# A routed mixture's end: 39 of 47 blocks summed during the last blocks, eight added in DRAM with their weights

## What is computed

```python
scores = softmax(xt @ Wg.T)                     # xt = layernorm(x), (1024, 256); 16 experts
topi   = top_k(masked, 4)                       # masked: the best 2 of 4 groups of 4 experts
weights = scores at topi
combine[t, topi] += weights
h = silu(xt @ W1[e]) * (xt @ W3[e])             # inner size 176
expert_out[e, t] = h @ W2[e].T
y = sum over e of expert_out[e, t] * combine[t, e]
z = silu(xt @ Ws1.T) * (xt @ Ws3.T) @ Ws2.T     # shared part
x = x + y + z
```

## Time and profile before

| | us |
|---|---|
| median of 3 runs (lowest, highest) | 798.14 (797.76, 800.05) |
| the profiled execution's own time | 797.48 |
| its span | 795.5 |
| PE busy, share of the span | 709.1, 89% |
| DVE busy | 574.2, 72% |
| ACT busy | 444.4, 56% |
| POOL busy | 399.1, 50% |
| mean granted TensorE clock | 0.961 |

### The profile page before, as it was taken

The page is one execution under the profiler, slowest core; times in us unless marked ns, Lnnn a source line. Parts: engine busy times, 40 slices in busy tenths (PEclk is TensorE's granted clock), DMA queues, the critical chain, the costliest instruction groups (busy, mean ns, idle before and its releaser), DMA issues. The chain is left out here.

```text
span 795.5 us, 12267 instructions
## 1 busy us (share of the span) xinstructions
PE 709.1 (89%) x3946; PEld 555.8 (70%) x3946; DVE 574.2 (72%) x1072; ACT 444.4 (56%) x969; POOL 399.1 (50%) x334
## 2 busy tenths in 40 slices
PE   8598967999999997999999999999798699999950
PEld 3144433688888886899998988988687555788840
DVE  6999999744343367889898888888889667544436
ACT  3887754253443335777776767776642266555530
POOL 0699877245675543534353232233232477777720
PEclk9699999999999998999999999999999799999975
DMA  4746411110444501120211033000077122233327
GB/s 142 281 168 254 163 64 44 59 37 22 140 129 133 175 14 48 41 73 27 74 60 34 22 105 139 1 1 1 21 275 263 40 67 87 87 100 101 100 80 231
DMA packets 38823, 77.66 MB, mean 98 GB/s; under 512 B 5345, under 2 KB 20394, under 8 KB 37738
## 3 DMA queue, kind: packets, MB, share of 16 engines
q1 hardware_dynamic: 34088, 64.41, 23.6%
q0 software_dynamic: 4512, 12.33, 5.1%
q10 hardware_dynamic: 162, 0.14, 0.1%
HBM read 59.07 MB, written 17.79 MB: 97 GB/s over the span
## 5 line engine op out<-in xcount | busy, mean ns | idle before, releaser
L1184 PE MATMUL psum<-xT_hi,w_ring 128*128 128x512 f32 x272 | 91.2, 395 | 1.0 <-ACTq L285 0.7
L2483 ACT ACTIVATE a_p_exp<-psum,a_nmax 128x256 f32<-128x256 f32 x128 | 59.6, 471 | 57.4 <-DVE a_nmax L2652 57.4
L2582 POOL TENSOR_TENSOR a_rr<-a_ss,eps 128x8 f32<-128x8 f32 x32 | 6.6, 206 | 158.0 <-DVE a_ss L2633 158.0
L641 POOL TENSOR_TENSOR m_dbu<-m_du,m_b_all 128x1024 f32<-128x1024 f32 x31 | 73.7, 2398 | 9.5 <-DVE m_du L727 6.9
L735 DVE TENSOR_TENSOR_SCAN m_hst<-psum,m_dbu 128x1024 f32<-128x1024 f32 x32 | 73.0, 2283 | 0.0
L1963 POOL DMA_INDIRECT expert_rows<-y_rows,f_puts_i x47 | 54.3, 1155 | 32.0 <-ACT y_rows L1909 31.4
L1320 POOL TENSOR_TENSOR f_h_lo<-f_hid,f_h_hi 128x512 fp32r<-128x512 f32 x34 | 44.0, 1296 | 44.6 <-ACT f_h_hi L1294 44.0
L2346 PE MATMUL psum<-a_kT,a_qT 128*128 128x256 f32 x256 | 62.0, 386 | 1.4 <-ACT a_kT L2475 1.4
L387 PE MATMUL psum<-m_hc,ident 128*128 128x512 f32 x128 | 61.8, 606 | 0.0
L1184 PEld LDWEIGHTS psum<-xT_hi,w_ring 128*128 128x128 f32 x272 | 51.1, 188 | 11.9 <-issue 1.5
L1294 ACT ACTIVATE f_h_hi<-f_hid 128x512 fp32r<-128x512 f32 x34 | 21.4, 631 | 63.3 <-DVE f_hid L1428 45.3
(11 more groups left out here) (312 smaller groups left out, 2245.7 us busy)
## 6 DMA issues: line engine op xcount, KB each, us to landing
expert<-in_experts SPq DMA_DIRECT2D x16, 608.0 KB, 8.6
m_b_all<-b_rows SPq DMA_DIRECT2D x8, 1024.0 KB, 5.9
w_raw<-in_moe SPq DMA_DIRECT2D x20, 384.0 KB, 3.5
k_raw<-m_side SPq DMA_DIRECT2D x16, 256.0 KB, 2.0
a_keys<-k_raw SPq DMA_DIRECT2D x16, 256.0 KB, 2.6
norm_rows<-xn SPq DMA_DIRECT2D x8, 512.0 KB, 7.6
added<-expert_rows SPq DMA_DIRECT2D x16, 256.0 KB, 5.7
fold_in<-in_w_fold SPq DMA_DIRECT2D x8, 384.0 KB, 3.3
```

The source lines that it names most:

```text
L641: pool.tensor_tensor(dbu[:, k % DBU_RING, :, :], du[:, h, :, :], b_all[:, n:n + 1, :].to_broadcast([P, G, HALF]), ALU.mult).then_inc(dbu_r ...
L1184: mm = pe.matmul(dst, a[part], b[of], start=(k == 0 and i == 0), stop=(k == KD - 1 and i == 2), skip_group_check=True)
L2483: ins = act.activation(pe_[:, n % 2, m, :], bank(hh)[:, tile * L:(tile + 1) * L], ACT.Exp, bias=nmax[:, n % 2, m:m + 1], accum_out=rsum[:, ...
```

## The change

Four things, with their places in the new kernel:

- **Exp and the weights move into the loop.** ACT takes Exp after turn 3, DVE makes the weights after turn 4 (WEIGHTS_AT = 4). SP then writes the weights to a DRAM array, slot_weights.
- **Eight weight gathers.** In turns 6 to 13 POOL fetches, for each of the last eight blocks, one number for each of its 128 rows. Their indices come from `lasts_listed`, nine DVE instructions ahead of block 0, and one more in `rows_listed`.
- **The last eight blocks (39 to 46)** are scaled by these weights in the y_rows copy, and their scatters add into two DRAM arrays in turn, last_rows0 and last_rows1, at the token's row. A scatter waits until the one before it in the same array has landed. The rows of expert_rows and of the two arrays are zeroed in the attention, by eight DMAs of 1 MB (8.4 MB in all), ahead of the first six experts in SP's queue (`sums_cleared`).
- **The end.** The first 39 blocks' rows are read once their scatters have landed, one token tile (four picks, 512 KB) a DMA, into two buffers in turn, xn and parts. A buffer is refilled when its tile has been added. DVE adds two picks in each of turns 43 to 46, the other 24 behind the loop, each waiting for the one before. Then SP reads the two arrays, four DMAs each, and DVE adds them in eight instructions of 512 columns.

```diff
 GATHERS = 6
+LAST = 8
...
-ADDED = [(f"added{k}", [P, NT, DM], F32) for k in range(4)]
+ADDED = [(f"added{p}", [P, NT, DM], F32) for p in range(2)]
...
+        self.inputs = 16 * (16 + 4 + 2 * 2)
+
+    def sums_cleared(self, sp):
+
+        zeros = self.sh.zeros[:, :].bitcast(F32)
+        first = T * 3 + P * (NB1 - LAST)
+
+        def cleared(rows):
+            sp.dma_start(rows.rearrange("(t p) f -> p t f", p=P),
+                         zeros.unsqueeze(1).to_broadcast([P, rows.shape[0] // P, DM])).then_inc(self.experts_in, 16)
+
+        for k in range(4):
+            cleared(self.d["y_rows"][k * T:(k + 1) * T, :])
+        for p in range(2):
+            cleared(self.d["last_rows"][p][0:T, :])
+            cleared(self.d["last_rows"][p][first:first + LAST * P, :])
...
+    KEPT = NB - LAST
+    WEIGHTS_AT, PARTS_AT = 4, KEPT + 4
...
+        parts = [sh.xn, sh.tables["parts"]]
...
-            return len(range(r, NB, PUTS))
+            return len(range(r, KEPT, PUTS))
...
+                sp.wait_ge(weights_kept, 1)
+                sp.dma_start(d["slot_weights"].rearrange("(p r) w -> p (r w)", p=P),
+                             weights_of[:, :, :].rearrange("p k t -> p (k t)")).then_inc(weights_out, 16)
                 for r in range(PUTS):
                     sp.wait_ge(put[r], 16 * puts_of(r))
+                for t in range(NT):
+                    if t >= 2:
+                        sp.wait_ge(final, picks * (t - 1))
+                    sp.dma_start(parts[t % 2][:, :, :],
+                                 d["y_rows"][0:picks * T, :].rearrange("(k t p) f -> t p k f", p=P, k=picks)[t]).then_inc(part_in[t % 2], 16)
+
+                def sums(p, q):
+                    return d["last_rows"][p][2 * q * P:(2 * q + 2) * P, :].rearrange("(t p) f -> p t f", p=P)
+
+                sp.wait_ge(y_s, NB)
+                sp.wait_ge(last_put[0], 16 * lasts_of(0))
                 for q in range(NT // 2):
-                    for k in range(picks):
-                        at = k * T + 2 * q * P
-                        sp.dma_start(added[k][:, 2 * q:2 * q + 2, :],
-                                     d["y_rows"][at:at + 2 * P, :].rearrange("(t p) f -> p t f", p=P)).then_inc(added_in[q], 16)
+                    sp.dma_start(added[0][:, 2 * q:2 * q + 2, :], sums(0, q)).then_inc(added_first, 16)
+                sp.wait_ge(last_put[1], 16 * lasts_of(1))
                 for q in range(NT // 2):
-                    sp.wait_ge(final, 2 * picks * (q + 1))
+                    sp.dma_start(added[1][:, 2 * q:2 * q + 2, :], sums(1, q)).then_inc(added_in[q], 16)
+                for q in range(NT // 2):
+                    sp.wait_ge(final, picks * NT + NT // 2 + q + 1)
                     sp.dma_start(out.rearrange("(t p) f -> p t f", p=P)[:, 2 * q:2 * q + 2, :],
                                  x[:, 2 * q:2 * q + 2, :]).then_inc(stored, 16)
                 sp.wait_ge(stored, 16 * (NT // 2))
...
                 def block_out(i):
                     act.wait_ge(y_ps, i + 1)
-                    if i >= PUTS:
+                    j = i - KEPT
+                    if j >= PUTS:
+                        act.wait_ge(last_put[j % 2], 16 * ((j - PUTS) // 2 + 1))
+                    elif i >= PUTS:
                         act.wait_ge(put[i % PUTS], 16 * (i // PUTS))
-                    act.activation(y_rows[:, i % PUTS, :], y_bank(i)[:, 0:DM], ACT.Copy).then_inc(y_s, 1)
+                    if j < 0:
+                        act.activation(y_rows[:, i % PUTS, :], y_bank(i)[:, 0:DM], ACT.Copy).then_inc(y_s, 1)
+                    else:
+                        if j == 0:
+                            act.wait_ge(slot_weights, 16 * LAST)
+                        act.activation(y_rows[:, i % PUTS, :], y_bank(i)[:, 0:DM], ACT.Identity, scale=slot_weight[:, j:j + 1])\
+                            .then_inc(y_s, 1)
...
-                act.wait_ge(weighed, 1)
-                act.activation(ex[:, :, :], ex[:, :, :], ACT.Exp).then_inc(mix.ex_ready, 1)
+                    if i == WEIGHTS_AT - 1:
+                        act.wait_ge(weighed, 1)
+                        act.activation(ex[:, :, :], ex[:, :, :], ACT.Exp).then_inc(mix.ex_ready, 1)
...
                 def scatter(i):
                     pool.wait_ge(y_s, i + 1)
+                    j = i - KEPT
+                    if j >= 0:
+                        if j >= 2:
+                            pool.wait_ge(last_put[j % 2], 16 * (j // 2))
+                        pool.indirect_dma_start(d["last_rows"][j % 2], bass.IndirectOffsetOnAxis(last_i[:, j:j + 1], 0),
+                                                y_rows[:, i % PUTS, :], None, compute_op=ALU.add).then_inc(last_put[j % 2], 16)
+                        return
                     pool.indirect_dma_start(d["y_rows"], bass.IndirectOffsetOnAxis(puts_i[:, i:i + 1], 0),
                                             y_rows[:, i % PUTS, :], None).then_inc(put[i % PUTS], 16)
 
                     if i + GATHERS - 1 < NB:
                         gather(i + GATHERS - 1)
                     scatter(i)
+                    if WEIGHTS_AT + 2 <= i < WEIGHTS_AT + 2 + LAST:
+                        j = i - WEIGHTS_AT - 2
+                        if j == 0:
+                            pool.wait_ge(rows_ready, 4)
+                            pool.wait_ge(weights_out, 16)
+                        pool.indirect_dma_start(slot_weight[:, j:j + 1], None, d["slot_weights"],
+                                                bass.IndirectOffsetOnAxis(weight_i[:, j:j + 1], 0)).then_inc(slot_weights, 16)
...
+                def lasts_listed():
+
+                    last = slice(KEPT, NB)
+                    step(dve.tensor_scalar(whole_row, row, -(T - 1) / 2, 1.0 / T, ALU.add, ALU.mult))
+                    step(dve.tensor_scalar(whole_row, whole_row, MAGIC, None, ALU.add))
+                    step(dve.tensor_scalar(whole_row, whole_row, -MAGIC, None, ALU.add))
+                    step(dve.scalar_tensor_tensor(whole_row, whole_row, -float(T), row, ALU.mult, ALU.add))
+                    dve.tensor_tensor(last_i[:, :], whole_row, rows_f[:, last], ALU.add).then_inc(rows_ready, 1)
+                    step(dve.tensor_scalar(whole_tile, row, -(P - 1) / 2, 1.0 / P, ALU.add, ALU.mult))
+                    step(dve.tensor_scalar(whole_tile, whole_tile, MAGIC, None, ALU.add))
+                    step(dve.tensor_scalar(whole_tile, whole_tile, -MAGIC, float(1 - P * picks * NT), ALU.add, ALU.mult))
+                    dve.scalar_tensor_tensor(weight_i[:, :], row, float(picks * NT), whole_tile, ALU.mult, ALU.add)\
+                        .then_inc(rows_ready, 1)
...
+                def part_added(part):
+
+                    t, k = part // picks, part % picks
+                    if k == 0:
+                        dve.wait_ge(part_in[t % 2], 16 * (t // 2 + 1))
+                    else:
+                        dve.wait_ge(final, part)
+                    dve.scalar_tensor_tensor(x[:, t, :], parts[t % 2][:, k, :], weights_of[:, k, t:t + 1], x[:, t, :],
+                                             ALU.mult, ALU.add).then_inc(final, 1)
...
-                weights_picked()
-                for q in range(NT // 2):
-                    dve.wait_ge(added_in[q], 16 * picks)
-                    for k in range(picks):
-                        if k > 0:
-                            dve.wait_ge(final, 2 * (picks * q + k))
-                        for t in (2 * q, 2 * q + 1):
-                            dve.scalar_tensor_tensor(x[:, t, :], added[k][:, t, :], weights_of[:, k, t:t + 1], x[:, t, :],
-                                                     ALU.mult, ALU.add).then_inc(final, 1)
+                    if i == WEIGHTS_AT:
+                        weights_picked()
+                    if PARTS_AT <= i < NB:
+                        part_added(2 * (i - PARTS_AT))
+                        part_added(2 * (i - PARTS_AT) + 1)
+
+                for part in range(2 * (NB - PARTS_AT), picks * NT):
+                    part_added(part)
+                dve.wait_ge(added_first, 16 * NT // 2)
+                for p in range(2):
+                    for q in range(NT // 2):
+                        if p == 0:
+                            dve.wait_ge(final, picks * NT)
+                        else:
+                            dve.wait_ge(added_in[q], 16)
+                            dve.wait_ge(final, picks * NT + q + 1)
+                        xs = x[:, 2 * q:2 * q + 2, :].rearrange("p t f -> p (t f)")
+                        dve.tensor_tensor(xs, xs, added[p][:, 2 * q:2 * q + 2, :].rearrange("p t f -> p (t f)"), ALU.add)\
+                            .then_inc(final, 1)
...
+                sparse.sums_cleared(sp)
```

28 lines of the change are left out of this document (22 added, 6 removed).

## The result

| | before | after |
|---|---|---|
| median (lowest, highest) | 799.1 (797.76, 800.44) | 820.12 (816.97, 822.72) |
| runs | 4 | 4 |
| ratio, 95% interval | | 1.0282 (1.0249 to 1.0314) |
| profiled execution: own time, span | 797.48, 795.5 | 820.04, 818.2 |
| E, end of the last y_rows copy | 769.5 | 791.9 |

The change makes the kernel 21 us slower. The forecast said slower, by 7; its range ended at 812. The loop costs more than forecast and the tail gives nothing. The ratios in this document leave out an execution that lies over 1.5% above the fastest of its kernel, and only one does: the profiled one of weights_ahead (819.24).

A forecast was written before the change was run, and what follows sets the result against it. PE nearly fills the loop, and every microsecond saved in the tail is span. 1.4 + 2.5 + 6.5 - 3.2 = +7.2 on 797.48 gives 804.7, with half the 0.66 to the median 805.0 us; range 798 to 812.

The forecast's parts named there:

- step 3: Blocks 6 to 13: eight weight gathers on POOL, 0.97 us each plus gap, make PE wait for rows: +6.5 us.
- step 5: Tail: part reads in two buffers, then the two arrays' reads and adds, end at E+22.8 instead of E+26.0: -3.2 us.
- step 2: Block 4: making the weights on DVE delays b_hidT, for which PE waits: +2.5 us.
- step 4: Zeros, list operations, early reads, adds in the loop and scaling of y_rows are all covered: no cost.
- Exp into the loop: ACT after block 3: Exp and table loads start the next gate late, on the path to PE's down product: +1.4 us.
- steps 1 and 2: Exp with its table loads on ACT and the weights on DVE, blocks 3 and 4: together +3.9 us.
- the rival of a stretched POOL: Weight gathers starting under DVE's experts_lo cost 1.5 us each, 4.4 more in all: 809 us, chance 0.2.
- the bound of -8: Tail: with every read early DVE sets the pace, and the arrays' reads end it at about E+18.
- slow adding scatters: Last blocks: serialised adding scatters slower than 5.3 us lengthen the chain, past 6.6 the tail waits; at 8, 810; chance 0.1.
- A fast weight gather and the bound in the tail: Weight gathers on POOL nearly free and the tail gains 8 us: 793 with no gather delay, chance 0.1.

The follow-up runs named there:

- weights_ahead: The changed kernel with Exp and the weights made ahead of block 0, weight gathers where they are: 811.2 us, ratio 1.0141 to the kernel before.
- the filled pauses: The changed kernel with matmuls of zeros before block 4's down product and before the x_rows transposes of turns 9 to 15: 816.83 us.
- four_part_buffers: The changed kernel with four part buffers instead of two, so that four tiles' reads are in flight, loop untouched: 814.55 us, ratio 1.0194.
- plain_last: The changed kernel with the last eight blocks' scatters writing plainly instead of adding, waits and order kept: 819.12 us, ratio 1.0250.

## Why the prediction was wrong

The direction was right, and so were the prices of the table load, Exp, the weights and one weight gather. The time was short by 15 us, and by the profiled executions the sum of +7.2 met 22.7. Of these 15.5 us, about 3.9 are step 3 (the weight gathers), 3.5 step 5 (the tail), 2.7 a term that the sum didn't have (the clock behind step 2's wait) and 1.3 what step 4 put at nothing, together with small losses elsewhere in the loop. The other 4.0 are the distance at block 0, mostly no effect of the change.

1. **Exp into the loop, +1.4: right.** The gate of block 4 is 1.4 us later than the copies ahead of it. The drain of 1.38 us that the Trainium skill gives (ScalarE: Activation LUTs, "What ACT_TABLE_LOAD costs") doesn't appear: Exp starts 0.01 us behind the load's end, the gate too. By it the sum would have been 2.8 us more; the filled pauses give 3.8 for steps 1 and 2, not 6.7.
2. **Weights, +2.5: right as a wait, short as a price.** b_hidT was 3.95 late. "Nothing later recovers it" was true, but more is lost later: PE had waited 3.58 us and its next matmuls ran at the lower clock, 2.8 us. No term of the sum had the clock. The rows of before could have warned: in the stretch ahead of block 0 (624 to 640 us), where PE is busy 10.74 of 16 us, the clock stood at 0.79.
3. **Weight gathers, +6.5: mis-sized, 10.4 here and up to 13.0 elsewhere.** The price of one was right (0.97 at least). POOL was 11.6 us late by block 19's row gather, where the step had 9.2: the eight took 10.7 with their gaps, not 10.2, the other DMAs 1.5 more than before, and they found 0.6 of free room, not 1.0. I had given the rival of a stretched POOL 0.2, since row gathers had never stretched. In the kernel before none starts while experts_lo runs; pushed from their place, two do (2.08 and 2.04 us). Then the step took off 0.9 for POOL's idle time ahead of 686.61, which lies behind block 19's row gather, and 1.7 for a gather's lead. That lead was misread: block 25's gather didn't land 2.72 us after its start.

```profile
L1958 POOL DMA_INDIRECT x_rows<-norm_rows,f_rows_i x1: 973/973/973, 698.5 to 698.5; - x1
...
DMA to landing us min/median/max: 3.6/3.6/3.6
```

So it had 0.8 us to spare, as block 17's had; block 19's had 1.9. The rows of block 19 came 11.6 - 1.9 = 9.7 late. PE was 10.4 late there, 0.7 more than these rows ask for, after the low clock from 700 to 706 us; in the other kernels without fillers the clock added up to 4.

4. **Covered edits at zero: the zeros and the adds on DVE right, the reads wrong.** I asked whether the two early reads land in time for DVE (they do: the adds in the loop start without a wait, at 780.00) and never whom they meet. They meet the last row gathers: block 45's took 5.1 us to land instead of 3.7, and it has 0.8 to spare. The Trainium skill (DMA: Bandwidth & Descriptors, "Queues, rings and completion order") has each DMA engine take packets from its queues in turn; that fits, though no run here separates queues. "Scaling y_rows leaves an ACTIVATE an ACTIVATE": it took 0.47 instead of 0.38 us, and cost nothing. The list instructions cost nothing that shows. That an adding scatter might hold POOL longer (1.56 instead of 0.99 us) stood in no step.
5. **The tail, -3.2: it came to +0.3.** Tile 7's read was issued at E+9.7 where I had E+8.4, since DVE came out of the loop 0.6 us later and the tiles' reads landed after medians of 3.9 and 4.2 us (xn and parts) instead of 3.7. Then the arrays: I had half of them landed 7 us after SP's first issue, so four adds could run while the rest came. The first add started 8.2 us after that issue (it waits for all four reads of the first array; the arrays' reads landed after a median of 6.7 us), and then eight stood in a row, 4.9 us. four_part_buffers comes near the bound of -8 that I named and didn't take, with DVE setting the pace: its tail is 19.3 instead of 26.0, -6.7.

Of the rivals, a stretched POOL was partly true; slow adding scatters were true in another way than I wrote. They land in 4.0 at the median, but two took 6.3 and 5.9, more than the chain's 5.3, and POOL waited 3.4 us for them. The tail didn't: the last had landed at E+4.8, and SP reads the arrays from E+10.2. What they cost is the 0.6 us longer that each held POOL. A fast weight gather and the bound in the tail didn't occur.

## What to carry over

Price a wait of PE by what it is and by what follows: read the granted clock behind the pauses that the profile already has. On an engine without room, an added instruction also moves the others, and one that is pushed under a conflict it used to miss gets longer. Before calling an early transfer hidden, list what else is in flight in that window and who waits for it, and read the lead of the very transfer that will be pushed (0.8 to 1.9 us here, by block). The cure was to start the early reads when the last row gather had landed, and to put the extra gathers, four instead of eight, where POOL was idle.

## What the runs showed of the hardware

- After PE waits of 3.57 or 3.58 us the next down product took 2.37 or 2.38 instead of 1.32 us, in seven kernels; matmuls of zeros in the pause kept it at 1.32, in two.
- The lower clock can outlast its cause by far: after waits of 1.2 and 3.1 us, PE, busy without a pause, stood at 0.50 for 10 us and more (780 to 790 us in plain_last and four_part_buffers), or not at all (the change itself, 1.00 after a wait of 1.10).
- What a POOL DMA takes depends on where it starts under DVE's experts_lo (1.43 us). By the start's distance from that of experts_lo, in the kernel before and the change: 0.16 to 0.20 us, 2.08 and 2.04; 0.27, 2.02; 0.45, 1.84; 1.03, 1.25; 1.10, 1.17. Such a row ends 2.2 to 2.3 us after experts_lo's start, whatever it is. One that starts before experts_lo keeps its 0.97, even if experts_lo starts 0.23 us into it. The other traces agree (weight gathers too), but for two row gathers of weights_ahead that start 0.02 us into it and keep 0.95.
- An indirect gather of 128 single numbers keeps POOL as long as one of 128 rows of 1 KB, 0.97 us; an adding scatter 1.56 against 0.99 for a plain one.
